# Two-layer graph network on one core: layer 1 opens with 16 tiles that leave the last pair of node blocks out, and six tiles of round 0 are gathered unscaled

## The reference

```python
# layer 0
out_deg = max(segment_sum(1, src), 1);  in_cnt = segment_sum(1, dst)
t1  = x @ W1
msg = (t1[src] + x[src] * x[dst] @ W2) / (sqrt(out_deg[src]) * sqrt(out_deg[dst]))
e   = where(in_cnt > 0, t1 + segment_sum(msg, dst), 0) + b
e   = leaky_relu(e, 0.01);  e = e / max(norm(e), 1e-12)
x1  = layernorm(x + e)
# layer 1
xt  = x1 @ W.T + b
out = segment_sum(xt[src], dst) / (segment_sum(1, dst) + 1)
result = layernorm(x1 + out)
```

## Time and profile before

| | us |
|---|---|
| median of 3 runs (3874.12, 3874.19, 3880.11) | 3874.19 |
| the profiled execution | 3876.01 |
| its span | 3874.2 |
| its granted TensorE clock, mean | 0.76 |
| POOL busy | 2893.6 (75%) |
| PE busy | 2712.6 (70%) |
| DVE busy | 1911.7 (49%) |
| gathers: kept, layer 0, layer 1 | 282, 1247, 1506 |

### The profile page before, as it was taken

The page is one execution under the profiler, slowest core; times in us unless marked ns, Lnnn a source line. Parts: engine busy times, 40 slices in busy tenths (PEclk is TensorE's granted clock), DMA queues, the critical chain, the costliest instruction groups (busy, mean ns, idle before and its releaser), DMA issues.

```text
span 3874.2 us, 65859 instructions
## 1 busy us (share of the span) xinstructions
PE 2712.6 (70%) x10186; PEld 1845.4 (48%) x10186; DVE 1911.7 (49%) x3812; ACT 498.1 (13%) x1540; POOL 2893.6 (75%) x3055
## 2 busy tenths in 40 slices
PE   4551777776767676766777777777777777777777
PEld 4440455555656565655634444444343444444443
DVE  8995466665666665666632333333333333333333
ACT  8992000000000000000000000000000000000000
POOL 7776777777777777777757777777777777777776
PEclk5555789888888888888866777777877877777777
DMA  8878455555555555555434444444444444444443
GB/s 255 271 239 314 150 163 164 164 165 164 164 163 166 164 164 163 165 161 164 147 96 122 126 129 125 130 124 130 127 129 126 129 126 129 128 127 130 126 130 108
DMA packets 326862, 597.16 MB, mean 154 GB/s; under 512 B 72525, under 2 KB 211330, under 8 KB 326498
## 3 DMA queue, kind: packets, MB, share of 16 engines
q0 software_dynamic: 145680, 398.00, 36.1%
q1 hardware_dynamic: 152952, 173.52, 13.6%
q10 hardware_dynamic: 27866, 22.52, 1.9%
HBM read 506.32 MB, written 75.50 MB: 150 GB/s over the span
## 4 chain that ended last, share of the span: by engine, by line
POOL 35%; issue 20%; SPq 20%; ACTq 6%; DMA 4%; PE 3%; DVE 1%; DVEq 1%; POOLq 0%; ACT 0%
POOL ring L652 35%; SPq L474 14%; ACTq L839 4%; SPq L467 3%; DMA ring<-x,idx 3%; PE banks L1463 2%; ACTq L816 1%; ACTq L864 1%; SPq L401 1%; DMA ring<-src_lo 1%; SPq L396 1%; SPq L447 1%; DMA x_t<-in_x 0%; SPq L454 0%; PE banks L1427 0%
## 5 line engine op out<-in xcount | busy, mean ns | idle before, releaser
L1463 PE MATMUL banks<-ring,hot_space 128*128 128x257 f32 x6252 | 2116.8, 476 | 594.4 <-DMA ring<-x,idx 468.1
L1463 PEld LDWEIGHTS banks<-ring,hot_space 128*128 128x128 f32 x6252 | 1288.1, 228 | 1355.2 <-DMA ring<-x,idx 943.5
L652 POOL DMA_INDIRECT ring<-x,idx x1506 | 1427.7, 948 | 481.5 <-issue 451.9
L652 POOL DMA_INDIRECT ring<-scaled_x,idx x1247 | 1191.3, 955 | 392.8 <-issue 381.5
L1160 DVE SCALAR_TENSOR_TENSOR big<-banks,here_mask,big 128x257 f32 x784 | 342.9, 479 | 1390.5 <-PE banks L1463 1384.4
L1106 DVE TENSOR_TENSOR hot_space<-banks,dst_rel 128x1024 f32<-128x1024 f32 x345 | 421.9, 1224 | 166.2 <-issue 164.5
L1416 PE MATMUL banks<-ident,halves 128*128 128x128 f32 x588 | 138.5, 392 | 384.5 <-DVE halves L1174 382.0
L663 POOL DMA_INDIRECT ring<-in_x,src_col x276 | 264.2, 957 | 84.1 <-issue 84.1
L1416 PEld LDWEIGHTS banks<-ident,halves 128*128 128x128 f32 x588 | 103.6, 203 | 424.7 <-DVE halves L1174 378.8
L729 ACT ACTIVATE dst_rel<-columns,halves 128x128 bf16<-128x128 f32 x960 | 268.3, 391 | 5.7 <-DVE halves L1019 5.7
L768 ACT COPY idx<-src_col 128x32 int32 (+1 forms) x97 | 21.1, 218 | 1844.6 <-issue 913.7
(11 more groups left out here) (126 smaller groups left out, 1167.7 us busy)
## 6 DMA issues: line engine op xcount, KB each, us to landing
src_lo<-x ACTq DMA_DIRECT2D x3648, 1.0 KB
src_lo<-x SPq DMA_DIRECT2D x3648, 1.0 KB
src_lo<-scaled_x SPq DMA_DIRECT2D x2944, 1.0 KB
kept_rows<-ring SPq DMA_DIRECT2D x94, 384.0 KB, 3.2
ring<-kept_rows SPq DMA_DIRECT2D x47, 768.0 KB
ring<-x,idx POOLq DMA_INDIRECT x1506, 4.3
src_lo<-scaled_x ACTq DMA_DIRECT2D x1408, 1.0 KB
ring<-scaled_x,idx POOLq DMA_INDIRECT x1247, 2.8
```

Source lines behind the costliest of these rows:

```text
L652: g.indirect_dma_start(ring[:, u, 0:D], None, table[layer], bass.IndirectOffsetOnAxis(ap=idx[:, idx_buf(layer, n), u:u + 1], axis=0)).then ...
L1463: last = nc.tensor.matmul(group_sum(k % SUMS), dst_hot[:, k % HOTS, u - k * GT, :], ring[:, u, 0:DW], start=u == tiles[0], stop=u == tiles ...
```

## The change

**First part, the end of layer 0.** The last pair is node blocks 96 and 97 (`LAST_NODE` and up). The sources of the first 16 tiles of layer 1 (`AHEAD_GROUPS` = 2 groups) are changed in `src_col`: an edge whose source is in the last pair gathers another row, and its destination is moved out of the window (`hide_last_pair`, `PITCH` added to the second copy of `dst_rel`), so it adds nothing. What it should have added is put back by TensorE: before layer 0 begins, `count_last_pair` counts for each of the two groups how many edges go from each node of the last pair to each destination, the counts go to memory (`pair_dram`), come back into `w2_s` when W2 is no longer needed, and `add_last_pair` multiplies them by the last pair's finished rows, with a column of ones. SP raises `table1_whole` twice: once when all pairs but the last are stored, once at the end. GpSimd gathers the 16 tiles after the first, the others after the second. VectorE finishes pair 47 wholly (moments and norm too) before the sums of the last two groups, and makes three `dst_hot` groups of layer 1 before it finishes the last pair.

**Second part, the start of layer 0.** The six first tiles of round 0 are gathered from the unscaled `x` straight into the ring, as soon as the three places of the staging area that lie under them are stored; `unit_place` turns the staging places so that the last units lie elsewhere. `find_r(0)` and `group_hot_scaled(0, 0)` scale them. Round 0 gathers 26 tiles instead of 32 from the table.

```diff
+AHEAD_GROUPS = 2
+AHEAD_TILES = AHEAD_GROUPS * GT
+LAST_NODE = (NW - 2) * P
+PLACE_TURN = UNITS - 1 - (KEPT_UNITS - 1) % UNITS
+RAW_PLACES = -(-(KEPT * PITCH) // (UNIT * D))
+PLACES_AT = BASES_AT + 2
@@ SP
+            def load_first_places():
+
+                sp.wait_ge(r_made, 1)
+                sp.dma_start(first_place_src, src[0:KE].rearrange("(a n) -> a n", a=1).to_broadcast([P, KE])
+                             ).then_inc(places_in, 16)
...
+                if n == PLACES_AT:
+                    load_first_places()
+            sp.wait_ge(counts_whole, 2)
+            sp.dma_start(pair_dram, pair_made).then_inc(ints_stored, 16)
             sp.wait_ge(ints_made, 2)
...
+            def pass_all_but_last(layer):
+
+                for s in range(2):
+                    sp.wait_ge(stored[s], 16 * ROUNDS)
+                sp.sem_inc(table1_whole, 1)
+                sp.wait_ge(projected, 2 * ROUNDS + 2)
+                sp.dma_start(w2_s[:, :, :].rearrange("p k n -> p (k n)"), pair_dram).then_inc(weights_loaded, 16)
...
             def load_places(i):
 
-                if not (isinstance(i, int) and i == 1):
-                    sp.wait_ge(places_made, i - 1)
+                sp.wait_ge(places_made, i)
...
                     next_pair(layer, ROUNDS - 2, last=True)
+                    if layer == 0:
+                        pass_all_but_last(layer)
@@ GpSimd
+                    rows = table[layer]
+                    if whole_at is not None and q < whole_at:
+                        rows = rows[0:LAST_NODE, :]
+                    if q == whole_at:
+                        g.wait_ge(table1_whole, 2)
...
-            for place in range(UNITS):
-                g.wait_ge(kept_out[place], 16 * len(range(place, KEPT_UNITS, UNITS)))
+            for place in range(RAW_PLACES):
+                g.wait_ge(kept_out[place], 16 * units_at(place))
+            for u in range(KEPT):
+                g.indirect_dma_start(ring[:, u, 0:D], None, x,
+                                     bass.IndirectOffsetOnAxis(ap=src_col[:, u:u + 1], axis=0)).then_inc(rows_in[u], 16)
+            for place in range(RAW_PLACES, UNITS):
+                g.wait_ge(kept_out[place], 16 * units_at(place))
...
-                    gather_round(layer, 0, 0, ahead=layer == 1)
+                    gather_round(layer, 0, 0, first=first, ahead=layer == 1, whole_at=AHEAD_GROUPS if layer else None)
@@ ACT
-                        act.wait_ge(table1_whole, 1)
+                        act.wait_ge(table1_whole, 2)
@@ VectorE
+            def count_last_pair():
+
+                tiles = [P, GT, P]
+                across = lane_row.unsqueeze(1).to_broadcast(tiles)
...
+                for n in range(AHEAD_GROUPS):
+                    rel = dst_rel[:, n * GT:(n + 1) * GT].unsqueeze(2).to_broadcast(tiles)
+                    nc.vector.tensor_tensor(dst_hot[:, n, :, :], across, rel, ALU.is_equal)
+                ordered()
+                for n in range(2 * AHEAD_GROUPS):
+                    if n >= 2:
+                        v.wait_ge(hot_used, SRC_BATCHES + n + 1)
...
+                    nc.vector.tensor_tensor(dst_hot[:, 2 + n % 2, :, :], across, sources,
+                                            ALU.is_equal).then_inc(hot_made, 1)
+                v.wait_ge(hot_used, SRC_BATCHES + 2 + 2 * AHEAD_GROUPS)
+                nc.vector.tensor_copy(pair_made, banks[:, 6, :]).then_inc(counts_whole, 1)
...
+            make_places(0, first_place_src, first_place_hot)
+            find_r(0)
+            ordered()
+            count_last_pair()
...
-                        if layer == 1:
-                            moments(layer, i - 1)
-                            norm(layer, i - 1)
+                        moments(layer, i - 1)
+                        norm(layer, i - 1)
...
                         mix(ENDS, acc[:, NW - 2:NW, :], x_last, mask_last[:, :], last=True)
-                        moments(layer, ENDS - 1)
-                        norm(layer, ENDS - 1)
+                        for n in range(2):
+                            nc.vector.memset(out_ones[n][:, D:DW], 1.0)
+                        for k in range(1, GR):
+                            group_hot(TILES + (k - 1) * GT, (k + AHEAD) % HOTS)
@@ TensorE
+            def count_last_pair():
+
+                for n in range(2 * AHEAD_GROUPS):
+                    pe.wait_ge(hot_made, SRC_BATCHES + n + 1)
+                    for t in range(GT):
+                        last = nc.tensor.matmul(pair_sums[:, n, :], dst_hot[:, 2 + n % 2, t, :], dst_hot[:, n // 2, t, :],
+                                                start=t == 0, stop=t == GT - 1)
+                    last.then_inc(hot_used, 1)
+
+            def add_last_pair(k):
+
+                pe.wait_ge(weights_loaded, 112)
+                for s in range(2):
+                    pe.wait_ge(out_ready[s], ROUNDS)
+                    rows = P if s == 0 else LAST_ROWS
+                    last = nc.tensor.matmul(group_sum(k % SUMS), pair_counts[0:rows, k, s, :], out_ones[s][0:rows, :],
+                                            start=False, stop=s == 1)
+                last.then_inc(groups_done, 1)
```

More of the change, by code:

```diff
@@ L139, in gnn @@
             "p (d t) -> p d t", d=2)
+        halves_flat = halves[:, :, :, :].rearrange("p s h f -> p (s h f)")
+        pair_made = halves_flat[:, 0:2 * AHEAD_GROUPS * P]
+        pair_src = [halves_flat[:, 2 * AHEAD_GROUPS * P + n * AHEAD_TILES:2 * AHEAD_GROUPS * P + (n + 1) * AHEAD_TILES]
+                    for n in range(2)]
         idx = sb("idx", [P, 2, U], I32)
@@ L185, in gnn @@
         mask_last = sb("mask_last", [P, 2])
-        out_last = [dst_col[:, n * D:(n + 1) * D] for n in range(2)]
+        out_ones = [dst_col[:, n * DW:(n + 1) * DW] for n in range(2)]
+        out_last = [out_ones[n][:, 0:D] for n in range(2)]
         wl_s = [a_t[n][:, 0, :, :] for n in range(2)]
@@ L204, in gnn @@
         project = [banks[:, 6, s * D:(s + 1) * D] for s in range(2)]
-        project_last = [banks[:, 0, s * D:(s + 1) * D] for s in range(2)]
+        project_last = [banks[:, SUMS - 1, s * D:(s + 1) * D] for s in range(2)]
+        pair_sums = banks[:, 6, :].rearrange("p (g n) -> p g n", n=P)
         found = banks[:, 4:6, 0:UNIT * NW].rearrange("p b (t n) -> p b t n", t=UNIT)
@@ L308, in node_no, with unit_place, units_at @@
             return layer * ROUNDS + m
+        def unit_place(n):
+            return (n + PLACE_TURN) % UNITS
+        def units_at(place):
+            return len(range((place - PLACE_TURN) % UNITS, KEPT_UNITS, UNITS))
         def idx_buf(layer, i):
@@ L641, in _, with gather_round @@
                                         base=offset, pattern=[[-1, P]], channel_multiplier=1).then_inc(consts_made, 1)
-            def gather_round(layer, i, n, end=U, first=0, ahead=True):
+            def gather_round(layer, i, n, end=U, first=0, ahead=True, whole_at=None):
                 g.wait_ge(idx_ready, layer * ROUNDS + i + 1)
@@ L650, in gather_round @@
                         g.sem_inc(gather_turn, 1)
+                    rows = table[layer]
[3 more added lines that the diff above has]
+                        g.wait_ge(table1_whole, 2)
                     for u in range(max(q * QT, first), min((q + 1) * QT, end)):
-                        g.indirect_dma_start(ring[:, u, 0:D], None, table[layer],
+                        g.indirect_dma_start(ring[:, u, 0:D], None, rows,
                                              bass.IndirectOffsetOnAxis(ap=idx[:, idx_buf(layer, n), u:u + 1],
@@ L693, in _ @@
                 g.wait_ge(sums_zeroed, 64)
+                for u in range(KEPT):
+                    g.wait_ge(rows_in[u], 16)
                 g.sem_inc(tile_over, 1)
@@ L906, in round_ @@
                     take_turned(layer, i - 1)
-                if last and layer == 0:
-                    norm_root(i - 1)
-                elif last:
-                    var_root(layer, i - 1)
+                if last:
+                    roots(layer, i - 1)
                 if hand is not None:
@@ L960, in _ @@
                     if layer == 0:
-                        var_root(layer, ENDS - 1)
                         for m in range(ENDS - 1, ROUNDS):
@@ L1145, in _ @@
                     nc.vector.memset(big[:, first * D:end * D], 0.0)
-            for g in range(AHEAD):
-                group_hot(g * GT, g)
+                if c == 2:
+                    group_hot_scaled(0, 0)
+                    for g in range(1, AHEAD):
+                        group_hot(g * GT, g)
             for place in range(UNITS):
-                v.wait_ge(kept_out[place], 16 * len(range(place, KEPT_UNITS, UNITS)))
+                v.wait_ge(kept_out[place], 16 * units_at(place))
             nc.vector.memset(ring[:, :, D:DW], 1.0).then_inc(ring_ones, 1)
@@ L1288, in _ @@
                     round_(layer, 0, False, False, layer == 0)
+                    if layer == 0:
+                        hide_last_pair()
```

(10 more changed lines are left out.)

50 lines of the change are left out of this document (36 added, 14 removed).

## The result

| | before | after |
|---|---|---|
| median of 5 runs, side by side on one chip | 3876.67 us (3874.12 to 3880.11) | 3855.09 us (3853.63 to 3859.34) |
| ratio, 95% interval | | 0.9946 [0.9935, 0.9956] |
| span of the profiled execution | 3874.2 us | 3853.3 us |
| first gather from the table | 372.63 | 374.97 |
| last gather of layer 0 | 1945.24 | 1941.64 |

The forecast was 3855.2 us for the median, a gain of 19.0 us. In the profiles the first gather of layer 1 is 18.6 us earlier, and the last gather 18.1 us; the span shrank by 20.9, because the tail behind the last gather took 17.1 us instead of 20.0.

The account below looks back on a forecast made before the run. GpSimd's stream of gathers was taken to bound the kernel, with SP close behind in layer 0. 14.3 + 7.5 - 1.4 - 0.3 - 1.1 = 19.0 us off the median of 3874.2 gave 3855.2 us, range 3850 to 3865.

Parts of the forecast that it names:

- The boundary: Between layers 0 and 1: the first gather of layer 1 comes 14.3 us earlier, at 1954.2 instead of 1968.5; bounds 11 to 15.
- The two pieces: Pair 47 at layer 0's end: 3.39 us from square root to norm, then 3.58 us from norm to GpSimd's first gather.
- The release of the 17th tile: Early layer 1: GpSimd's release for the whole table comes at 1972.6, 1.6 us ahead of the 17th tile's due time, 1974.2.
- SP's wait in layer 1: SP's row copies lose 18 us of slack, so its long wait shrinks from 45.6 to near 28 us.
- 17th tile waits: Rival, early layer 1: the second release comes after 1974.2 and each us is lost; 3859 to 3862 us; chance 0.12.
- no early start: Rival, end of layer 0: something the early gathers need comes only then, the 14.3 us are gone; 3873.6 us; chance 0.06.
- slower: Rival: SP's row copies pace both layers, layer 1 starts 4.1 us later and layer 0 pays 1.1; 3879.4 us; chance 0.05.
- The front: Start of layer 0: six gathers leave round 0, gaining 7.5 us, less 1.4 for transfers and 0.3 for casts; bounds 2 to 7.5.
- VectorE's passes in front of the loop: Before layer 0: two new integer passes delay GpSimd's gathers by 0 to 2.4 us, taken as 0.3.
- The transfers: Before layer 0: 0.9 MB of new traffic on full DMA engines delays the last kept store by 0 to 2.4 us, taken as 1.4.
- SP's extra register step: SP's loop in layer 0: one more register value per two rounds, some 0.06 us over 19 passes, costs 1.1 us; bounds 0 and 3.
- SP keeps the front's gain: Rival, layer 0: SP's full stretch begins no earlier, so GpSimd waits at its ring's limit; 3861 us; chance 0.19.

Follow-up runs that it names:

- the end alone: Changed kernel with the early gathers of round 0 taken back, so only the end of layer 0 is changed: 3859.81 us, ratio 0.9961 to the kernel before.
- e3: Changed kernel with only 8 tiles of layer 1 instead of 16 gathered on the first release: 3861.14 us, ratio 0.9965 to the kernel before.
- r1: The changed kernel profiled again with nothing altered: 3854.23 us.
- r3: The changed kernel a third time with nothing altered, in a second session: 3860.10 us, ratio 0.9951 to the kernel before.
- front-only kernel: Changed kernel with release, counts and order of the last pairs as before, so only layer 0's start is changed: 3873.45 us, ratio 0.9997; run again, 3872.27 us.

## Why the prediction was right, point by point

**The boundary, 14.3 us: right.** The pause shrank by 14.96 us; 14.3 with the end alone. The two pieces of which the working made it, 3.39 and 3.58 us, measured 3.39 and 3.64. The release of the 17th tile was forecast 1.6 us ahead of its time and came about 2.5 us ahead. The last pair's mix did move behind pair 47's norm (3.1 us after it began, 3.8 forecast). Of the rest all stayed hidden: the counts' load at 1957.58, `add_last_pair` at 1964.22, and SP's wait in layer 1 of 27.6 us, where 28 were forecast. The rivals "17th tile waits", "no early start" and "slower" fall with that, and e3 shows how the first of them would have looked.

**The front, 7.5 - 1.4 - 0.3 us: right in kind, short in size.** The start should have come 1.7 us later and came 2.3 us later (1.5 to 2.3 over three executions). The two terms can be told apart. VectorE's passes in front of the loop were put at 0.3 us, and the last kept gather ends at 362.29 instead of 362.02. The transfers were put at 1.4 us, and the last kept store landed 2.5 us later: 0.7 because it was issued later, 1.8 because it took longer. That the full DMA engines did it fits their 379 GB/s, but no run takes the transfers away while it keeps the rest. VectorE had 3.6 us to spare. Of 7.5 us, 5.2 are there at the start.

**SP's extra register step, 1.1 us: it is there, and doesn't show.** From 550 to 1680 the trace has 17 register operations for this wait before (L453) and 35 after (L494), and the next instruction starts some 0.07 us behind one. So its size was about right, 1.3 us over 19 passes. But it can't be seen in the period (64.45 before, 64.44, 64.42 and 64.36 after), nor at GpSimd: over the three executions it waits 1.4, 0.2 and 0.0 us in layer 0 beyond its usual 0.30 us per gather, where 2.2 us stood before and near 4 were forecast. Taking the 1.1 us off GpSimd's gain was the mistake. The chance that SP keeps the front's gain was put at 0.19; it falls too: SP's first pass is at 466.96 instead of 471.74, 4.8 us earlier, as the gathers are. At 534.61 only 2.0 are left in this execution, since there TensorE's products for the pair took 5.30 us and SP waited for the rows; in r1 they took 3.62 us and the pass is at 531.63. Two windows of the timeline give the difference (busy by engine, granted clock, DMA share, GB/s), the changed kernel's first, r1's second:

```profile
511.00:517.00 6.00, 6.00 (x20) 5.00 (x21) 3.82 (x6) 0.00 (x0) 4.48 (x6) 0.72 0.38 101
```

```profile
511.00:517.00 6.00, 6.00 (x30) 5.29 (x29) 3.34 (x5) 0.00 (x0) 4.48 (x6) 1.00 0.41 110
```

The granted clock was at its full 2.4 GHz in r1 and partly at 1.2 GHz in the other. In the 11 us before, TensorE was busy for 7.47 us in r1 and for 5.85 in the other; but in r3, with 7.32 us, the products took 5.30 us too, so I can't say what decides it. The first two end layer 0 within 1.2 us of each other: it cost little.

**What the working left out: longer gathers.** From the start to the last gather of layer 0 the gain falls from 5.2 to 3.6 us. 2.3 us of it are excess in the gathers' own durations (14.2 against 11.9), and 0.8 come back as shorter waits. I had put 0.3 us for VectorE's passes in the prelude and nothing for the rounds. The two errors, 1.1 us for SP that GpSimd hardly felt and 1.5 us for gathers that were missing, cancelled: 14.96 + 3.6 = 18.6 at the first gather of layer 1, against 19.0 forecast, and 18.1 at the last. That was luck. It was luck too that the median came within 0.1 us of 3855.2: the gain was 21.6 us instead of 19.0, and the median of the kernel before, 3874.2 when the forecast was made, was 3876.7 beside the changed kernel. In the profiles the span fell by 20.9 and not by 18.1 because of before's long tail (2.9 us: the last rows took 4.79 us to land instead of 3.37, and the last products 3.80 instead of 3.33), which no step of the change touches. I can't show more than that it is absent from every other profiled execution.

**Which gathers are longer** is seen when gathers above 1.0 us are set beside VectorE's timeline. One of each kind from the changed kernel, GpSimd first:

```profile
999.33 1.09 POOL L700 DMA_INDIRECT ring<-scaled_x,idx  x1 [0.30 <-issue]
...
1023.22 1.11 POOL L700 DMA_INDIRECT ring<-scaled_x,idx  x1 [0.30 <-issue]
```

```profile
999.04 0.55 DVE L1175 TENSOR_SCALAR dst_col<-dst_col 128x768 int32<-128x768 int32 x1
999.68 0.62 DVE L1177 TENSOR_SCALAR dst_col<-dst_col,lane 128x768 f32<-128x768 int32 x1
...
1023.03 0.48 DVE L1264 SCALAR_TENSOR_TENSOR halves<-x_t,root,big 128x256 f32<-128x256 f32 x1
1023.43 0.42 DVE L1266 TENSOR_TENSOR halves<-x_t,big 128x256 f32<-128x256 f32 x1
```

They last 0.16 us more on average, 87 times in the changed kernel's layer 0. Not every meeting counts: of its 247 gathers that overlap the integer passes, the mix (the two lines at 1023) or the sum of squares of a pair, 79 are long. In all twelve profiled executions together 1135 of 14904 gathers of layer 0 are longer than 1.0 us. None of them is among the 2646 that VectorE's work didn't overlap at all, and none among the 3401 that overlap `add_group` (L1252), a `scalar_tensor_tensor` that reads one of its two inputs from a bank of TensorE's results instead of SBUF.

Beside the sum of squares (L1286) the moment decides. Of the gathers that began 0.5 to 0.3 us ahead of it, 101 of 101 were long, by 0.2 us for most; of those that began at most 0.1 us ahead of it, 0 of 120. Since gathers and VectorE's work repeat with nearly the same period, it is a matter of phase which moment they meet. In the front-only kernel 36 and 38 long gathers overlap the sum of squares (7.1 and 6.9 us in its two executions), in the changed kernel 13, 14 and 10 (2.1, 2.3 and 1.5 us), in the kernel before 14 (2.0 us). The difference of some 5 us is most of what the front-only kernel loses against before. That explains its loss by size; it isn't tested by a run that shifts the phase alone, and why the phase falls so in one kernel and otherwise in another was not tried.

**What stays open.** How the time splits between the parts isn't settled by the times: 3859.81 with the end alone against 3855.09 and 3860.10 for the changed kernel in two sessions, with overlapping ratios. The front's 2.6 to 3.1 us rest on the positions of gathers in three profiles against one, and the pause alone differs between executions of the changed kernel by 1.0 us (8.2 to 9.2).

## What to carry to other kernels

When one engine's stream of equal pieces sets the time, write down where it stops and what releases it, and move the release, not the work. A wait for "all of it" can often be split so that the first pieces go on with a part; size the part so that the rest is due just after its release, as 16 tiles were here and 8 were not. Where a second engine is within a microsecond per two rounds of the first, look for what shifts with the gain: here SP waits early for the gathers and so moved with them.

## What the hardware showed that I had not expected

- **Gathers are lengthened by VectorE work that isn't a copy.** In the rows above a gather took 1.11 us instead of 0.95 beside `tensor_tensor` and `scalar_tensor_tensor` with two inputs in SBUF, and 1.09 beside integer passes. Of the 3401 gathers that overlap `add_group`, with one input in a bank, none was lengthened. Of those that overlap the mix or the integer passes more than half aren't either. The sum over layer 0 was 11.9 to 19.8 us, and 2.6 to 4.7 us in layer 1, where fewer such operations run. The Trainium skill ("SBUF — State Buffer", Who interferes with whom) says that an instruction with two SBUF inputs contends with GpSimd instructions that read SBUF. The gathers read their indices from SBUF (`idx`), and the rows agree that they are lengthened; but 0.16 us on average is far from a gather held for the whole operation of 0.42 to 0.48 us.
- **A step of SP's queue that does nothing takes 0.059 us**, 0.70 for twelve, and yet twelve of them lengthened SP's period by 0.43 us only, because the pause at its loop's end got shorter (3.03 us instead of 3.23 to 3.35).
- **SP loses about 3.3 us at the end of each pass of its loop** in layer 0: its branch stands at 599.8 and the next instruction at 603.0 (L597). It waits for nothing that the profile shows there.
- **The tail behind the last gather varies by 4 us** (16.3 to 20.0) between twelve executions whose code for it is the same; 20.0 was seen once, and without it they vary by 1.2 us.
